# Sliding-window attention on Trainium2: masked-out quarter blocks of the local scores left out of matmul, exp and mask

## The chip, the cores and the metric

One Trainium2 chip, all 8 cores of it. Each core computes two of the sixteen sequences on its own, with the same program; there is no communication. The metric is the device time of one launch in microseconds, that of the slowest core.

## The reference

The input is 16 sequences of 2048 tokens with 1024 features. First comes an attention layer, then a feed-forward part with three pairs of 1024x1024 matrices that are dequantized from 4 bits. The change touches the local attention alone:

```python
def _local_window_attn(Q, K, V):          # 16 heads of 64, window W = 256
    Qb = Q.reshape(Bx, H, nb, W, D)
    ...
    Kw = jnp.concatenate([Kp[:, :, :-1], Kp[:, :, 1:]], axis=3)   # block before, own block
    Vw = jnp.concatenate([Vp[:, :, :-1], Vp[:, :, 1:]], axis=3)
    i = jnp.arange(W)[:, None]
    j = jnp.arange(2 * W)[None, :]
    base = (j > i) & (j <= i + W)
    ...
    sc = jnp.where(mask[None, None], sc, -jnp.inf)
    p = jax.nn.softmax(sc, axis=-1)
    out = jnp.einsum('bhnij,bhnjd->bhnid', p, Vw)
```

Query i of a block of 256 sees keys i+1 to i+256 of the 512 keys of the block before and its own block. A second, pooled ("latent") attention over 64 positions is added with gates, then the output projection and the residual.

## The kernel before

Everything is one program in `build_program`, with one queue per engine and semaphores written out by hand: te counts PE, sc ScalarE (ACT), ve VectorE (DVE). Each engine runs its instructions strictly in the order of the code, so that order is also the order of the work. The first phase (up to about 2014 us) is attention, the second the feed-forward part. The change lies in the first.

The first phase runs over 16 tiles of 256 tokens: `ti` 0 to 15, the first 8 of one sequence, the last 8 of the other. A tile does, in this order: K projection (L461), the latent query projection (L470), gates (L477), pooled keys and values (L557 to L572), the latent attention (scores L622, exp L634, mask L642, product L661, normalized by L678), then the local attention in four groups of four heads, `hf` = 0 to 3, then V and Q projections of the next tile (`emit_vq`, L386 and L415), and the output projection (L893).

Keys lie in chunks of 128: kc = 0, 1 are the block before, kc = 2, 3 the own block. Scores are kept transposed, 128 keys on the partitions and 256 queries along the row. For one `hf`:

- PE, scores (L774): for each kc and each pair of heads two matmuls of 256 query columns into one half (512 columns of f32) of the upper part of psA. Two such halves alternate; the third block waits until the exp of the first has been read out (`t.wait_ge(sc.h, sc0 + nb - 1)`).
- ACT, exp (L796): one 128x512 activation per block, from psA into the buffer expP in SBUF.
- DVE, mask (L808): one 128x512 multiplication per block with the mask `mlocS` of that kc, in place, each followed by a drain (L811) whose end is counted.
- PE, AV (L835, L838): when all masks of the hf are done, for each half of the queries (qc = 0, 1 of 128 each), each of the 4 heads and each kc a matmul of 64 columns with the values and one of 1 column with ones, which sums the row. qc = 0 goes to psB and psC, qc = 1 to psA and psD.

This makes 8 blocks per hf. In tiles 0 and 8, the first of a sequence, there is no block before: kc is only 2 and 3, 4 blocks per hf.

The masks, from the host code, with m1 and m2 triangles of 128x128:

```python
mloc[0] = np.concatenate([m1, zeros_t], axis=1)
mloc[1] = np.concatenate([ones_t, m1], axis=1)
mloc[2] = np.concatenate([m2, ones_t], axis=1)
mloc[3] = np.concatenate([zeros_t, m2], axis=1)
```

What stands between the groups matters too. After the scores, exps and masks of hf = 0 comes `emit_remote_tail`: the latent result is transposed by DMA (SP's queue, L251), projected on PE (L725), copied out by ACT (L736, Copy), and transposed by DMA again. PE's AV of hf = 0 waits for those copies. Then `emit_remgate` on DVE: a wait for the second transposes, and two pairs of gate multiplications (L692, L696); the masks of hf = 1 come behind it in DVE's order. Before hf = 2 stands `emit_ln1_xf` of the next tile: statistics on DVE (L320 to L326), Sqrt on ACT (L337), scaling on DVE (L345, L347), and DMA transposes. ACT loads a table each time that it changes its function (the table load carries the line of the activation behind it). After hf = 3 DVE mixes both attentions, qc = 0 first (L853, L855, L860, L864), then qc = 1; PE goes on with V's projection, 16 matmuls for each half of the tokens (`tc`), where the second half waits for DVE's copies (L397) of the first, and these stand behind the mixing in DVE's order.

Of the kernel before, what the change touches and what calls it, by code (L numbers as in the profile page):

```python
# [11 lines left out]
AF = mybir.ActivationFunctionType  # L12
# [13 lines left out]
TILE = 256  # L26
# [42 lines left out]
def build_program():  # L69
# [30 lines left out]
    with contextlib.ExitStack() as es:  # L100
# [14 lines left out]
        mlocS = sb("mlocS", [128, 4 * 256], BF16)  # L115
# [14 lines left out]
        o_QF = A(H * TILE)  # L130
# [58 lines left out]
        sc = Sem(es, nc, "sc")  # L189
# [51 lines left out]
        def I(sem, inst, k=1):  # L241
            sem.n += k
            inst.then_inc(sem.h, k)
            return sem.n
# [191 lines left out]
        for ti in range(min(B * NT, DBG_A_TILES)):  # L436
# [314 lines left out]
            kc_all = [2, 3] if n == 0 else [0, 1, 2, 3]  # L751
            for hf in range(4):
                if hf == 2 and ti + 1 < B * NT:
                    emit_ln1_xf(ti + 1)
                te_sb = {}
                sc_exp = {}
                sregs = [psA[:, 1024:1536], psA[:, 1536:2048]]

                @block.tensor
                def _(t, hf=hf, slot=slot, pslot=pslot, n=n, kc_all=kc_all):  # L760
                    t.wait_ge(ve.h, kg_evac)
                    sc0 = sc.n
                    nb = 0
                    for kc in kc_all:
                        sl = pslot if kc < 2 else slot
                        koff = (kc % 2) * 128
                        for hg in range(2):
                            reg = sregs[nb % 2]
                            if nb >= 2:
                                t.wait_ge(sc.h, sc0 + nb - 1)  # L770
                            mm = None
                            for hh in range(2):
                                h = hf * 4 + hg * 2 + hh
                                mm = t.matmul(  # L774
                                    reg[:, hh * 256:(hh + 1) * 256],
                                    ar_t.ap()[0:64,
                                              o_KR + h * 2 * W + sl * W + koff:
                                              o_KR + h * 2 * W + sl * W + koff + 128],
                                    ar_t.ap()[0:64,
                                              o_QF + h * TILE:o_QF + (h + 1) * TILE],  # L780
                                    start=True, stop=True)
                            te_sb[nb] = I(te, mm)
                            nb += 1

                nbt = len(kc_all) * 2

                @block.scalar
                def _(s, hf=hf, kc_all=kc_all, nbt=nbt):
                    for nb in range(nbt):
                        s.wait_ge(te.h, te_sb[nb])  # L790
                        reg = sregs[nb % 2]
                        kc = kc_all[nb // 2]
                        hg = nb % 2
                        dst = ar_t.ap()[:, o_expP + kc * 4 * TILE + hg * 2 * TILE:
                                        o_expP + kc * 4 * TILE + (hg + 1) * 2 * TILE]
                        sc_exp[nb] = I(sc, s.activation(dst, reg, AF.Exp))  # L796

                @block.vector
                def _(v, hf=hf, kc_all=kc_all, nbt=nbt):
                    for nb in range(nbt):  # L800
                        v.wait_ge(sc.h, sc_exp[nb])
                        kc = kc_all[nb // 2]
                        hg = nb % 2
                        dst = ar_t.ap()[:, o_expP + kc * 4 * TILE + hg * 2 * TILE:
                                        o_expP + kc * 4 * TILE + (hg + 1) * 2 * TILE]
                        mkv = mlocS.ap()[:, kc * 256:(kc + 1) * 256].unsqueeze(1) \
                            .broadcast_to((128, 2, 256))
                        v.tensor_tensor(dst.rearrange("p (g q) -> p g q", g=2),   # L808
                                        dst.rearrange("p (g q) -> p g q", g=2), mkv,
                                        op=ALU.mult)  # L810
                        I(ve, v.drain())  # L811
                locexp_done = ve.n

                if hf == 0:
                    emit_remote_tail()
                    emit_remgate()

                @block.tensor
                def _(t, hf=hf, slot=slot, pslot=pslot, n=n, kc_all=kc_all):
                    t.wait_ge(ve.h, locexp_done)  # L820
                    if hf == 0:
                        t.wait_ge(ve.h, remnorm_done)
                        t.wait_ge(sc.h, rem_marks['rempf'])
                    for qc in range(QC):
                        avreg = psB[:, 0:1024] if qc == 0 else psA[:, 0:1024]
                        dreg = psC[:, 0:16] if qc == 0 else psD[:, 0:16]
                        for hh in range(4):
                            h = hf * 4 + hh
                            for ki, kc in enumerate(kc_all):
                                st = ar_t.ap()[:, o_expP + kc * 4 * TILE + hh * TILE + qc * 128:  # L830
                                               o_expP + kc * 4 * TILE + hh * TILE + qc * 128 + 128]
                                vsl = (slot * 2 + kc - 2) if kc >= 2 else (pslot * 2 + kc)
                                first = ki == 0
                                last = ki == len(kc_all) - 1
                                mmA = t.matmul(avreg[:, h * 64:(h + 1) * 64], st,  # L835
                                               V(o_VR + vsl * 1024 + h * 64, 64),
                                               start=first, stop=last)
                                mmB = t.matmul(dreg[:, h:h + 1], st,  # L838
                                               onesS[:, 0:1], start=first, stop=last)
                        I(te, mmA)  # L840
                        mix_marks[(hf, qc)] = I(te, mmB)
# [837 lines left out]
```

## Time and profile before

| | us |
|---|---|
| median of the timed runs (2 runs, 4090.43 and 4103.03) | 4096.73 |
| profiled execution, its own time | 4023.44 |
| its span, slowest core (core 3) | 4021.9 |
| spans of the other cores | 4003.5 to 4016.2 |
| PE busy, matmuls | 2496.1 |
| DVE busy | 1923.8 |
| ACT busy | 1168.5 |

The trace is of one execution, on core 3, with times in us from the start of the span. A row of the timeline gives the start, the duration, the engine, the line of the code, output and input by name with their shapes, and in brackets how long the engine stood idle before it and what ended that. xN at the end merges N instructions that follow each other. PEld is the loading of weights, DVEq and ACTq are the drains of those engines. PEclk is the granted clock of TensorE as a share of 2.4 GHz.

### The profile page before, as it was taken

The numbers are of one execution on the slowest core, as the hardware profiler recorded it, in microseconds if no ns is written. First come the engines' busy times: TensorE is split into PE (matmuls) and PEld (weight loads), VectorE is DVE, ScalarE is ACT, GpSimd is POOL, SyncE is SP. The second block draws the span as 40 slices with busy tenths as digits, with TensorE's granted clock in tenths as the row PEclk, the third lists the DMA queues.
The fourth block names the chain that finished last, engine by engine and source line by source line (L and its number), as shares of the span: only waits on it lengthen the run. The fifth ranks groups of instructions, "written<-read, shape, count | busy, mean of one in ns | idle before, by whom it ended". The sixth has DMA issues, their size and how long they took to land.

```text
span 4021.9 us, 57687 instructions; the slowest of 8 cores (4003.5 to 4021.9 us)
## 1 busy us (share of the span) xinstructions
PE 2496.1 (62%) x20176; PEld 1594.7 (40%) x20176; DVE 1923.8 (48%) x3815; ACT 1168.5 (29%) x1873; POOL 88.4 (2%) x142
## 2 busy tenths in 40 slices
PE   0566665666755666665534656758485765848675
PEld 0344433444433444443311434435353443525343
DVE  0455544555544445544423454545444444545454
ACT  0122333222323222233345322313232322323232
POOL 1000000000000000000011000000000000000000
PEclk9767766767665677766656888879787887979788
DMA  9012111112111111111233010010202001020201
GB/s 141 14 30 33 25 30 30 30 30 33 25 35 30 30 30 30 30 27 30 32 86 91 1 35 19 6 48 1 53 1 53 1 17 36 3 51 1 48 1 32
DMA packets 259707, 128.20 MB, mean 32 GB/s; under 512 B 229232, under 2 KB 233504, under 8 KB 259424
## 3 DMA queue, kind: packets, MB, share of 16 engines
q1 hardware_dynamic: 224512, 62.94, 8.8%
q0 software_dynamic: 34912, 61.57, 7.2%
q8 instruction: 167, 2.74, 0.3%
q14 instruction: 116, 0.95, 0.1%
HBM read 61.99 MB, written 25.17 MB: 22 GB/s over the span
## 4 chain that ended last, share of the span: by engine, by line
PE 42%; DVE 26%; ACT 11%; issue 9%; DMA 5%; another core or an unknown queue 2%; DVEq 2%; SPq 1%; ACTq 1%; POOLq 0%; POOL 0%
PE psA L1276 7%; PE psA L1460 5%; PE psB L1460 5%; DMA arena<-arena 3%; ACT arena L796 3%; PE psA L774 3%; DVE arena L1403 3%; DVE arena L1397 3%; DVE arena L1383 2%; PE psA L386 2%; PE psA L461 2%; DVE arena L808 2%; ACT arena L1417 2%; PE psB L893 2%
## 5 line engine op out<-in xcount | busy, mean ns | idle before, releaser
L1276 PE MATMUL psA<-arena,wbig 128*128 128x256 bf16 x3072 | 472.3, 305 | 62.7 <-DVEq L1305 62.6
L1276 PEld LDWEIGHTS psA<-arena,wbig 128*128 128x128 bf16 x3072 | 298.2, 107 | 179.1 <-issue 98.1
L774 PE MATMUL psA<-arena 64*128 64x256 bf16 x960 | 250.7, 392 | 169.9 <-ACT arena L796 169.8
L808 DVE TENSOR_TENSOR arena<-arena,mlocS 128x512 bf16<-128x512 bf16 x480 | 204.1, 425 | 228.2 <-ACT arena L796 204.4
L1302 DVE TENSOR_SCALAR arena<-psA,biasS 128x256 bf16<-128x256 f32 x384 | 185.9, 484 | 246.1 <-PE psA L1282 196.1
L796 ACT ACTIVATE arena<-psA 128x512 bf16<-128x512 f32 x480 | 261.0, 595 | 59.7 <-PE psA L774 58.5
L547 ACT ACT_TABLE_LOAD x16 | 20.5, 1283 | 688.8 <-PE psC L477 688.8
L1460 PE MATMUL psA<-arena,wbig 128*128 128x256 bf16 x1536 | 218.7, 290 | 0.0
L386 PE MATMUL psA<-wbig,arena 128*128 128x512 bf16 x512 | 137.7, 431 | 129.6 <-DMA arena<-arena 120.6
L1460 PE MATMUL psB<-arena,wbig 128*128 128x256 bf16 x1536 | 201.1, 274 | 0.0
L774 PEld LDWEIGHTS psA<-arena 64*128 64x128 bf16 x960 | 73.7, 107 | 319.2 <-issue 309.9
L1417 ACT ACTIVATE arena<-arena,lnbS,lngS 128x256 bf16<-128x256 bf16 x384 | 194.6, 589 | 0.6
L1364 ACT ACT_TABLE_LOAD x48 | 61.6, 1283 | 445.4 <-DVEq L1357 445.3
L1432 PE MATMUL psC<-arena,laS 128*32 128x256 bf16 x384 | 63.4, 320 | 198.8 <-ACT arena L1417 198.8
L835 PE MATMUL psB<-arena 128*128 128x64 bf16 x960 | 80.8, 210 | 146.9 <-DVEq L811 129.7
L1417 ACT ACT_TABLE_LOAD x48 | 61.6, 1283 | 355.9 <-DVEq L1406 355.9
L1460 PEld LDWEIGHTS psA<-arena,wbig 128*128 128x128 bf16 x1536 | 142.3, 103 | 52.4 <-issue 15.3
L1244 PE MATMUL psC<-arena,laS 128*32 128x256 bf16 x384 | 56.5, 296 | 167.8 <-DMA arena<-arena 147.0
L1460 PEld LDWEIGHTS psB<-arena,wbig 128*128 128x128 bf16 x1536 | 134.6, 98 | 36.2
L835 PEld LDWEIGHTS psB<-arena 128*128 128x128 bf16 x960 | 74.3, 122 | 172.7 <-issue 172.7
L1311 ACT ACT_TABLE_LOAD x48 | 61.6, 1283 | 258.6 <-DVEq L1305 258.6
L796 ACT ACT_TABLE_LOAD x64 | 82.1, 1283 | 185.3 <-PE psA L774 184.9
(169 smaller groups left out, 4463.0 us busy)
## 6 DMA issues: line engine op xcount, KB each, us to landing
y<-arena POOLq DMA_DIRECT2D x16, 1024.0 KB, 4.5
arena<-qT POOLq DMA_DIRECT2D x48, 256.0 KB, 2.6
arena<-x_in POOLq DMA_DIRECT2D x16, 512.0 KB, 7.0
x2scr<-arena SPq DMA_DIRECT2D x16, 512.0 KB, 3.0
arena<-x2scr POOLq DMA_DIRECT2D x16, 512.0 KB, 7.7
arena<-arena SPq DMA_TRANSPOSE x224, 3.2
wbig<-wq POOLq DMA_DIRECT2D x1, 2048.0 KB, 18.2
wbig<-wk POOLq DMA_DIRECT2D x1, 2048.0 KB, 29.9
```

The source lines that it names most:

```text
L386: mm = t.matmul(reg, V(o_XF + c * TILE + tc * 128, 128), wv_(o_wv + c * 1024 + og * 512, 512), start=(c == 0), stop=(c == NCH - 1))
L461: mm = t.matmul(reg, wv_(o_wk + c * 1024 + oc * 128, 128), V(o_XF + c * TILE, TILE), start=(c == 0), stop=(c == NCH - 1))
L774: mm = t.matmul(reg[:, hh * 256:(hh + 1) * 256], ar_t.ap()[0:64, o_KR + h * 2 * W + sl * W + koff: o_KR + h * 2 * W + sl * W + koff + 128] ...
L796: sc_exp[nb] = I(sc, s.activation(dst, reg, AF.Exp))
L808: v.tensor_tensor(dst.rearrange("p (g q) -> p g q", g=2), dst.rearrange("p (g q) -> p g q", g=2), mkv, op=ALU.mult)
L835: mmA = t.matmul(avreg[:, h * 64:(h + 1) * 64], st, V(o_VR + vsl * 1024 + h * 64, 64), start=first, stop=last)
L1276: t.matmul(reg, wTv(i0, c, oc * 128, 128), V(hin_o + c * TILE, TILE), start=(c == 0), stop=False)
L1302: v.tensor_scalar(V(y1o + oc * TILE, TILE), Y1REGS[oc % 4], biasS[:, i0 * 8 + oc:i0 * 8 + oc + 1], None, ALU.add)
L1397: v.tensor_tensor(V(y1o, NCH * TILE).rearrange("p (c t) -> p c t", c=NCH), V(y1o, NCH * TILE).rearrange("p (c t) -> p c t", c=NCH), mv, op ...
L1403: v.tensor_tensor(V(go, NCH * TILE).rearrange("p (c t) -> p c t", c=NCH), V(y1o, NCH * TILE).rearrange("p (c t) -> p c t", c=NCH), iv, op= ...
L1417: I(sc, s.activation(V(go + c * TILE, TILE), V(go + c * TILE, TILE), AF.Gelu, bias=lnbS[:, sbk * 8 + c:sbk * 8 + c + 1], scale=lngS[:, sbk ...
L1460: t.matmul(reg, wTv(i1, c, oc * 128, 128), V(go + c * TILE, TILE), start=(c == 0), stop=False)
```

## The change

In chunk 0 the mask is zero for the upper 128 queries, in chunk 3 for the lower 128. The change leaves these parts out everywhere, and multiplies by the mask only where it has a triangle:

- scores: in blocks of kc = 0 and 3 each of the two matmuls has 128 columns instead of 256;
- exp: in those blocks the activation runs over two pieces of 128 (one per head), 128x2x128 instead of 128x512;
- mask: in every block (kc = 0 to 3) only the query half with the triangle is multiplied, 128x2x128 instead of 128x512; the halves of kc = 1 and 2 whose mask is all ones are no longer touched;
- AV: kc = 0 is left out for qc = 1 and kc = 3 for qc = 0, with the `start` and `stop` flags of the sums moved accordingly. Of 64 matmuls per hf 48 stay (in tiles 0 and 8 of 32, 24).

The number of blocks, their order, and all waits and counts stay the same.

```diff
--- before.py
+++ after.py
@@ -764,6 +764,7 @@
                     for kc in kc_all:
                         sl = pslot if kc < 2 else slot
                         koff = (kc % 2) * 128
+                        lq = 0 if kc == 0 else (1 if kc == 3 else None)
                         for hg in range(2):
                             reg = sregs[nb % 2]
                             if nb >= 2:
@@ -771,13 +772,16 @@
                             mm = None
                             for hh in range(2):
                                 h = hf * 4 + hg * 2 + hh
+                                q0c = 0 if lq is None else lq * 128
+                                qn = TILE if lq is None else 128
                                 mm = t.matmul(
-                                    reg[:, hh * 256:(hh + 1) * 256],
+                                    reg[:, hh * 256 + q0c:hh * 256 + q0c + qn],
                                     ar_t.ap()[0:64,
                                               o_KR + h * 2 * W + sl * W + koff:
                                               o_KR + h * 2 * W + sl * W + koff + 128],
                                     ar_t.ap()[0:64,
-                                              o_QF + h * TILE:o_QF + (h + 1) * TILE],
+                                              o_QF + h * TILE + q0c:
+                                              o_QF + h * TILE + q0c + qn],
                                     start=True, stop=True)
                             te_sb[nb] = I(te, mm)
                             nb += 1
@@ -793,7 +797,15 @@
                         hg = nb % 2
                         dst = ar_t.ap()[:, o_expP + kc * 4 * TILE + hg * 2 * TILE:
                                         o_expP + kc * 4 * TILE + (hg + 1) * 2 * TILE]
-                        sc_exp[nb] = I(sc, s.activation(dst, reg, AF.Exp))
+                        if kc in (0, 3):
+                            lq = 0 if kc == 0 else 1
+                            d3 = dst.rearrange("p (g q) -> p g q", g=2)[
+                                :, :, lq * 128:(lq + 1) * 128]
+                            r3 = reg.rearrange("p (g q) -> p g q", g=2)[
+                                :, :, lq * 128:(lq + 1) * 128]
+                            sc_exp[nb] = I(sc, s.activation(d3, r3, AF.Exp))
+                        else:
+                            sc_exp[nb] = I(sc, s.activation(dst, reg, AF.Exp))
 
                 @block.vector
                 def _(v, hf=hf, kc_all=kc_all, nbt=nbt):
@@ -801,13 +813,14 @@
                         v.wait_ge(sc.h, sc_exp[nb])
                         kc = kc_all[nb // 2]
                         hg = nb % 2
+                        mq = 0 if kc in (0, 2) else 1
                         dst = ar_t.ap()[:, o_expP + kc * 4 * TILE + hg * 2 * TILE:
                                         o_expP + kc * 4 * TILE + (hg + 1) * 2 * TILE]
-                        mkv = mlocS.ap()[:, kc * 256:(kc + 1) * 256].unsqueeze(1) \
-                            .broadcast_to((128, 2, 256))
-                        v.tensor_tensor(dst.rearrange("p (g q) -> p g q", g=2), 
-                                        dst.rearrange("p (g q) -> p g q", g=2), mkv,
-                                        op=ALU.mult)
+                        d3 = dst.rearrange("p (g q) -> p g q", g=2)[
+                            :, :, mq * 128:(mq + 1) * 128]
+                        mkv = mlocS.ap()[:, kc * 256 + mq * 128:kc * 256 + mq * 128 + 128] \
+                            .unsqueeze(1).broadcast_to((128, 2, 128))
+                        v.tensor_tensor(d3, d3, mkv, op=ALU.mult)
                         I(ve, v.drain())
                 locexp_done = ve.n
 
@@ -824,14 +837,16 @@
                     for qc in range(QC):
                         avreg = psB[:, 0:1024] if qc == 0 else psA[:, 0:1024]
                         dreg = psC[:, 0:16] if qc == 0 else psD[:, 0:16]
+                        live = [kc for kc in kc_all
+                                if not ((kc == 0 and qc == 1) or (kc == 3 and qc == 0))]
                         for hh in range(4):
                             h = hf * 4 + hh
-                            for ki, kc in enumerate(kc_all):
+                            for ki, kc in enumerate(live):
                                 st = ar_t.ap()[:, o_expP + kc * 4 * TILE + hh * TILE + qc * 128:
                                                o_expP + kc * 4 * TILE + hh * TILE + qc * 128 + 128]
                                 vsl = (slot * 2 + kc - 2) if kc >= 2 else (pslot * 2 + kc)
                                 first = ki == 0
-                                last = ki == len(kc_all) - 1
+                                last = ki == len(live) - 1
                                 mmA = t.matmul(avreg[:, h * 64:(h + 1) * 64], st,
                                                V(o_VR + vsl * 1024 + h * 64, 64),
                                                start=first, stop=last)
```

The sizes on ACT, from the latent exps of tile 1 to the Copy evacuations behind hf = 0 (psA holds the scores, psD the projected latent result), before:

```order
L634 ACTIVATE arena<-psA 64x256 x8
L215 UNCONDITIONAL_BRANCH
L796 ACTIVATE arena<-psA 128x512 x8
L215 UNCONDITIONAL_BRANCH
L736 ACTIVATE arena<-psD 128x128 x2
```

and with the change, the same place:

```order
L634 ACTIVATE arena<-psA 64x256 x8
L215 UNCONDITIONAL_BRANCH
L806 ACTIVATE arena<-psA 128x2x128 x2
L808 ACTIVATE arena<-psA 128x512 x4
L806 ACTIVATE arena<-psA 128x2x128 x2
L215 UNCONDITIONAL_BRANCH
L736 ACTIVATE arena<-psD 128x128 x2
```

The eight exps stay eight, at the same place; the first two and the last two are of the half size. On PE, from the end of AV of hf = 0 to the start of AV of hf = 1 in tile 1, before:

```order
L838 MATMUL psD<-onesS,arena 128x1
L215 UNCONDITIONAL_BRANCH
L774 MATMUL psA<-arena 128x256 x16
L215 UNCONDITIONAL_BRANCH
L835 MATMUL psB<-arena 128x64
```

and with the change:

```order
L853 MATMUL psD<-onesS,arena 128x1
L215 UNCONDITIONAL_BRANCH
L777 MATMUL psA<-arena 128x128 x4
L777 MATMUL psA<-arena 128x256 x8
L777 MATMUL psA<-arena 128x128 x4
L215 UNCONDITIONAL_BRANCH
L850 MATMUL psB<-arena 128x64
```

Nothing changes its place here either; the outer blocks have narrower matmuls. The lines of the changed kernel behind the scores are shifted: L774 is L777, L796 is L806 and L808, L808 is L823, L835 is L850, L838 is L853.

## Rows read from the trace of the kernel before

**Rows 1.** The page of the kernel before: its span and the engines' busy time.

```profile
span 4021.9 us, 57687 instructions; the slowest of 8 cores (4003.5 to 4021.9 us)
...
PE 2496.1 (62%) x20176; PEld 1594.7 (40%) x20176; DVE 1923.8 (48%) x3815; ACT 1168.5 (29%) x1873; POOL 88.4 (2%) x142
```

**Rows 2.** Groups by line: shape, count | busy us, mean ns | idle before, releaser.

```profile
L796 ACT ACTIVATE arena<-psA 128x512 bf16<-128x512 f32 x480 | 261.0, 595 | 59.7 <-PE psA L774 58.5 <-issue 0.3
...
L774 PE MATMUL psA<-arena 64*128 64x256 bf16 x960 | 250.7, 392 | 169.9 <-ACT arena L796 169.8
...
L808 DVE TENSOR_TENSOR arena<-arena,mlocS 128x512 bf16<-128x512 bf16 x480 | 204.1, 425 | 228.2 <-ACT arena L796 204.4 <-issue 23.9
...
L634 ACT ACTIVATE arena<-psA 64x256 bf16<-64x256 f32 x128 | 41.3, 372 | 18.1 <-PE psA L622 17.9
...
L642 DVE TENSOR_TENSOR arena<-arena,mlatS 64x256 bf16<-64x256 bf16 x128 | 36.2, 283 | 121.9 <-ACT arena L634 108.8 <-issue 13.1
...
L563 PE MATMUL psD<-wbig,arena 128*8 128x128 bf16 x256 | 29.9, 311 | 0.0
```

**Rows 3.** Timeline, tile 5, hf = 2 and 3: start us, us, engine line.

```profile
805.55 1.09 ACT L796 ACTIVATE arena<-psA 128x512 bf16<-128x512 f32 x2
...
806.29 1.07 PE L774 MATMUL psA<-arena 64*128 64x256 bf16 x4 [2.91 <-ACT arena L796]
...
806.97 1.09 ACT L796 ACTIVATE arena<-psA 128x512 bf16<-128x512 f32 x2 [0.33 <-PE psA L774]
...
811.12 0.42 DVE L808 TENSOR_TENSOR arena<-arena,mlocS 128x512 bf16<-128x512 bf16 x1 [0.19 <-ACT arena L796]
...
811.72 0.21 PE L835 MATMUL psB<-arena 128*128 128x64 bf16 x1 [1.52 <-DVEq L811]
...
814.35 1.03 PE L774 MATMUL psA<-arena 64*128 64x256 bf16 x4
...
816.33 1.09 ACT L796 ACTIVATE arena<-psA 128x512 bf16<-128x512 f32 x2
```

**Rows 4.** Timeline, hf = 0 of tile 0, then hf = 0 to 2 of tile 5.

```profile
182.00 1.09 ACT L796 ACTIVATE arena<-psA 128x512 bf16<-128x512 f32 x2
...
185.43 1.01 PE L725 MATMUL psD<-arena,wbig 128*128 128x256 bf16 x4 [1.62 <-DMA arena<-arena]
...
771.51 1.09 ACT L796 ACTIVATE arena<-psA 128x512 bf16<-128x512 f32 x2
...
776.16 1.01 PE L725 MATMUL psD<-arena,wbig 128*128 128x256 bf16 x4
...
777.25 1.28 ACT L736 ACT_TABLE_LOAD   x1 [0.39 <-PE psD L725]
...
791.42 0.17 DVE L692 TENSOR_TENSOR rr<-glgrT,rden 128x16 f32<-128x16 f32 x1 [13.90 <-DMA arena<-arena]
...
794.83 0.43 DVE L808 TENSOR_TENSOR arena<-arena,mlocS 128x512 bf16<-128x512 bf16 x1 [0.19 <-issue]
...
799.12 0.42 DVE L808 TENSOR_TENSOR arena<-arena,mlocS 128x512 bf16<-128x512 bf16 x1 [0.19 <-issue]
...
804.04 0.20 ACT L337 ACTIVATE sigv<-stat 128x1 f32<-128x1 f32 x1 [0.66 <-DVEq L329]
```

**Rows 5.** Timeline, end of tile 4: mixing (DVE) and V projection (PE).

```profile
702.90 0.26 DVE L853 RECIPROCAL rl<-psC 128x16 f32<-128x16 f32 x1 [1.79 <-PE psC L838]
...
703.84 4.77 PE L386 MATMUL psA<-wbig,arena 128*128 128x512 bf16 x16
...
709.27 3.40 PE L386 MATMUL psA<-wbig,arena 128*128 128x512 bf16 x15 [0.66 <-DVE arena L397]
```

**Rows 6.** Windows, core 3: length, busy of PE, PEld, DVE, ACT, POOL, clock, DMA share, GB/s.

```profile
825.00:829.00 4.00, 4.00 (x16) 1.52 (x14) 3.52 (x6) 0.00 (x0) 0.00 (x0) 0.50 0.00 0
...
829.00:861.00 32.00, 28.14 (x232) 22.21 (x230) 20.78 (x47) 0.00 (x0) 0.00 (x0) 1.00 0.18 34
...
889.00:946.00 57.00, 33.69 (x369) 18.59 (x370) 23.88 (x54) 29.93 (x56) 0.00 (x0) 0.56 0.20 24
```

## The prediction

> **What bounds the kernel now.** I read the page's totals first, then the groups by line, then the timeline of tile 5 in order of time, then the windows for the granted clock. No engine is busy for more than 62% of the 4021.9 us span (PE) or 48% (DVE) [rows 1]. So a removed instruction is worth something only where its engine is the one that the next stage waits for, and the timeline has to say where that is. All that the change touches lies in the 64 head groups of the attention part (16 tiles, 4 groups hf = 0 to 3 each). 14 tiles have all four key chunks (I call them full), tiles 0 and 8 only chunks 2 and 3. Each group is a string of scores, exp, mask and AV, but which link of it the next stage waits for differs from group to group.
>
> The string in hf = 2 and 3 of tile 5 [rows 3]. Exps come in pairs; a pair takes 1.09 us and the next starts 1.42 us after it (805.55 to 806.97). The reader is to see why: PE may refill a PSUM half only when its exp has ended, so a period is one exp (0.60), 0.14 to PE's start at 806.29, and 0.68 for two matmuls until the next exp at 806.97. Four pairs make this 5.35 us. The last mask starts at 811.12, 5.57 us after the first exp, and ends 6.00 after it; AV starts 0.17 us later (released by DVE's drain), its 64 matmuls take until 814.35, 40 ns each, and the next group's scores and table load follow until the exp at 816.33.
>
> hf = 0 and 1 are tied otherwise [rows 4]. In hf = 0 the path leaves the exps early: L725 follows the last scores in PE's own order (776.16), and ScalarE's Copy evacuations wait for it (0.39 us at 777.25); masks and AV of hf = 0 are covered. Then DVE waits 13.90 us for the transposes (791.42), does four gate operations and only then the 8 masks of hf = 1, 0.613 us apart (794.83 to 799.12, 7 steps), while their exps are long done: DVE is the path. AV of hf = 1 is covered, since the LN statistics follow on DVE and the exps of hf = 2 wait for Sqrt, which waits for DVE (804.04).
>
> Behind hf = 3 the path is DVE again, not PE [rows 5]: the mixing starts at 702.90 when the first half of AV (qc = 0) is done, and V's second half (709.27) waits 0.66 us for DVE's copy. That is 6.4 us from the start of the mixing, the pattern repeats at each of the 15 changes of tile, and the second half of AV is covered by it.
>
> **The change part by part.** The new sizes do not stand in the trace, so each is bounded. *Exp, 2x128 instead of 512 elements:* 595 ns for 512, 372 ns for 256 at L634, on 64 partitions [rows 2]. Ends: 298 (half) and 595 (the two pieces cost as before). I take 372, the nearest row: same function, same PSUM source. *Mask, 2x128:* 425 ns for 512, 283 for 256 at L642 [rows 2]. Ends: 212 and 425. From the two durations of that kind I take 0.29, so 0.48 with the 0.19 between masks instead of 0.613: 0.13 less. *Scores, two matmuls of 128 columns:* L563 has 311 ns for 128 columns, L774 392 for 256 [rows 2]. At the 0.50 clock of this stage [rows 6] 128 columns are 107 ns, so two matmuls give 0.21 at most, 0 at least; I take 0.20. *AV:* of 64 matmuls 16 go, at 40 ns 0.64 us, 0.32 of it in the qc = 0 half; in tiles 0 and 8 half of that. No DMA and no wait is added, and each semaphore count stays.
>
> The string with these numbers, from the first exp on, for hf = 2 or 3 of a full tile: exp 2 at 0.37+0.14+0.68 = 1.20; exp 4 at 1.20+1.42 = 2.62; exp 6 (half scores) at 2.62+0.60+0.14+0.48 = 3.84; its mask at 3.84+0.37+0.10 = 4.31, the last mask at 4.80, its end 5.09. Before 6.00: **0.91 less**. The sum per full tile:
> hf = 0: first scores 0.20, then the last score block may start when exp 5 has ended, 0.22 earlier, and is itself 0.20 shorter: 0.62. This stays on the path only if the transposes that L725 needs have landed. In tile 0, with its short hf = 0, they are late: L725 waits 1.62 us for them [rows 4] and starts 3.4 us after the first exp (185.43 - 182.00); in tile 5 it starts 4.65 us after (776.16 - 771.51). 0.62 fits into the 1.2 us between.
> hf = 1: 8 masks x 0.133 = 1.07.
> hf = 2: 0.91, and AV 0.64: 1.55. Its first scores are covered by the LN statistics.
> hf = 3: first scores 0.20, 0.91, AV's qc = 0 half 0.32: 1.43.
> Together 4.67 us, x 14 = 65.4. Tiles 0 and 8: hf = 0 nothing (transposes), hf = 1 4 x 0.133 = 0.53, hf = 2 0.68+0.32, hf = 3 0.68+0.16, together 2.37, x 2 = 4.7 (0.68 is the same string with two pairs). The last tile has no LN of a next tile between, so AV of hf = 1 and the first scores count there: 0.64+0.20 = 0.8. **Sum 70.9, say 71 us.** The projections and the whole second phase are untouched.
>
> What is costed at nothing: AV of hf = 0 and 1 (14 x about 1.2 us) is hidden by DVE's wait for the transposes and by the masks and LN statistics; the second AV half of hf = 3 by DVE's mixing; the masks of hf = 0 by the Copy evacuations. Were those covers gone, some 21 us more would come (rival 3).
>
> The profiled execution took 4023.4 us, and its span is the base of this sum; the median of the timed runs is 4096.7, 1.8% more. 71 us of the former is 1.76%. I take the same 71 us off the median: **4026 us**.
>
> A rule on ScalarE's price. By the Trainium skill (ScalarE: Activation LUTs, What ACT_TABLE_LOAD costs) an ACTIVATE with immediate operands takes 186 ns and 0.833 ns per element, so 399 ns for 256 and 613 for 512. The row for 512 says 595, so the rule is a little high here. By it the exps would give some 2 us less in all.
>
> **The rivals.**
> 1. Masks cost as before (425 ns): the fixed part or the two pieces eat the half. Against it: 283 ns at L642. Then hf = 1 loses 1.07 and hf = 2 and 3 0.27 each: 3.06 per full tile, in all 46 us: 4050.
> 2. Exps cost 595 ns in two pieces. For it: no strided activation that reads PSUM stands in my rows. The last exp then comes at 4.55, the last mask ends at 5.54 (0.46 less), hf = 0 gives 0.40: 3.55 per full tile, in all 54 us: 4042.
> 3. The covered parts count too: 0.6 (AV of hf = 0), 0.64 and 0.32 more per full tile, 21 us: 92 us, 4005. Against it stand DVE's 13.90 us wait and V's 0.66 us wait for DVE [rows 4, 5].
> 4. Slower: the clock. In attention PE is granted 0.56 of full speed (889 to 946), at the head of the V projection still 0.50 (825 to 829), and 1.00 from there (829 to 861) [rows 6]; PE was busy without a gap for 4.00 us before it rose, and AV ran directly ahead of that. With a quarter of AV gone and shorter scores the rise could come later in each tile. K and output projections (64 matmuls of 256 columns) would need 107 ns a matmul at 2.4 GHz (1.00) and 213 at 1.2 GHz (0.50), so each would take 6.8 us more, Q and V by my estimate some 8 together: 21 us per tile if the clock never rose, 315 us in all, 4341. Break-even with my 4.67 us is a rise about 9 us later in each tile. Against it: V's 32 dense matmuls follow without a gap in any case, and the first half of V has spare time behind DVE's mixing.
> That half speed is the default and sustained activity releases it is also what the Trainium skill says (TensorE: Matmul & The Clock Gate, Part 1, the HAM clock gate). The trace agrees, 0.50 then 1.00; the rule speaks for rival 4 as a direction, not as a size.
>
> **How the numbers follow.** Forecast 0.65, rival 1 0.07, rival 2 0.10, rival 3 0.14, rival 4 0.04. A measurement here tells about 2% from no change, 82 us. Of the forecast's own spread (scores' 0.20 and the spread of the medians, 4090 to 4103) some 0.08 lies beyond 82 us, with rival 3 that is 0.22 faster; 0.04 slower; 0.74 within 2%. The forecast's own range is 4010 to 4045; the range given holds rivals 1 to 3 and the scatter of a median: 3998 to 4068. All upper prices at once would leave only AV's share, some 14 us (4083), which I leave out.
>
> **What would show it.** The group of half exps at about 372 ns, masks at 0.29 us with starts 0.48 apart in hf = 1 (3.85 us for eight, now 4.72), last mask 5.1 us after the first exp in hf = 2 and 3, AV in 48 matmuls and 2.0 us; V's second half still 6.4 us behind the mixing's start; L725 in full tiles released by PE's order and not by a DMA; tile period shorter by 4.7 us; second phase unchanged. I am wrong if the half operations cost over 0.45 us, if L725 turns to waiting for the transposes, or if the window behind V's start shows 0.50 for longer than now.

## The result and the profile after

The changed kernel took **3991.76 us** in the median of 18 runs, against 4025.28 us for the kernel before in 17 runs of the same rounds: ratio 0.987, 95% interval 0.9835 to 0.9904. That is faster, by less than 2%. Some executions of either kernel run with one die or both at a lower granted clock (about 0.70 to 0.745 in place of 0.75) and take up to 2.7% longer: 12 of the 18 of the changed kernel here against, by their times, 5 of the 17 of the kernel before, and 2 of 6 against 5 of 16 in the second timing, so the medians include them, the ratios leave out the clearest, and where a profile has one only the other die is compared. The six shortest times of the changed kernel (3948 to 3959 us) and the twelve shortest of the kernel before (4020 to 4030) are 68 us apart by their medians; why the first timing of the changed kernel has so many longer ones stays open. In a second timing (below) it was 3956.2 against 4022.3 us, ratio 0.9818, 0.9761 to 0.9876; the intervals overlap.

4026 us had been predicted, with a range from 3998 to 4068. The measured time lies 6 us below the range. The gain itself had been put at 71 us; the medians differ by 33.5 and 66 us, the spans of the profiles by 65 and 71 us.

The page of the changed kernel, the totals:

```profile
span 3954.3 us, 55767 instructions; the slowest of 8 cores (3942.1 to 3954.3 us)
...
PE 2424.0 (61%) x19216; PEld 1563.6 (40%) x19216; DVE 1859.8 (47%) x3815; ACT 1124.1 (28%) x1873; POOL 88.5 (2%) x142
```

The spans by core (core 0 is the shortest, core 3 the longest):

```profile
core 0: 3942.1 us, clock 0.757
...
core 3: 3954.3 us, clock 0.751
...
die 0 (median of its cores): 3947.5 us, clock 0.754
...
die 1 (median of its cores): 3946.0 us, clock 0.754
```

The mean of the eight spans is 3947.0 us; before it was 4011.9 us: 64.9 us less. PE lost 72 us of busy time, DVE 64 and ACT 44 [rows 1], 180 us in all, for 65 us of time.

The groups by line with the shapes kept apart (line, engine, operation, shapes, count | busy us, mean ns | idle before); they answer to [rows 2]:

```profile
L808 ACT ACTIVATE arena<-psA 128x512 bf16<-128x512 f32 x240 | 130.4, 595 | 49.1 <-PE psA L777 49.0
...
L806 ACT ACTIVATE arena<-psA 128x256 bf16<-128x256 f32 x240 | 86.2, 384 | 15.5 <-PE psA L777 0.8
...
L823 DVE TENSOR_TENSOR arena<-arena,mlocS 128x256 bf16<-128x256 bf16 x480 | 140.4, 292 | 218.8 <-ACT arena L806 105.2 <-ACT arena L808 82.4 <-issue 31.2
...
L777 PE MATMUL psA<-arena 64*128 64x256 bf16 x480 | 123.3, 395 | 145.8 <-ACT arena L806 122.4 <-ACT arena L808 23.4
...
L777 PE MATMUL psA<-arena 64*128 64x128 bf16 x480 | 79.2, 288 | 46.8 <-ACT arena L808 39.1
```

The exp in two pieces takes 384 ns (taken: 372), the mask 292 (taken: 290), a matmul of 128 columns is 107 ns shorter than one of 256. The profile shows the two pieces merged as 128x256.

The timeline of tile 5, hf = 2 and the start of hf = 3, answering to [rows 3]:

```profile
789.88 0.66 ACT L806 ACTIVATE arena<-psA 128x256 bf16<-128x256 f32 x2
...
791.08 1.09 ACT L808 ACTIVATE arena<-psA 128x512 bf16<-128x512 f32 x2 [0.55 <-PE psA L777]
...
794.68 0.29 DVE L823 TENSOR_TENSOR arena<-arena,mlocS 128x256 bf16<-128x256 bf16 x1 [0.20 <-ACT arena L806]
...
795.15 0.21 PE L850 MATMUL psB<-arena 128*128 128x64 bf16 x1 [1.05 <-DVEq L824]
...
797.14 0.61 PE L777 MATMUL psA<-arena 64*128 64x128 bf16 x4
797.61 1.28 ACT L806 ACT_TABLE_LOAD   x1 [3.03 <-PE psA L777]
798.90 0.66 ACT L806 ACTIVATE arena<-psA 128x256 bf16<-128x256 f32 x2
```

From the first exp (789.88) to the end of the last mask (794.97) it is 5.09 us, as forecast; before it was 6.00. AV with its 48 matmuls lasts from 795.15 to 797.14, 2.0 us instead of 2.6, and the next first exp follows the scores after 1.76 us instead of 1.98.

hf = 0 and 1 of tile 5, answering to [rows 4]:

```profile
763.78 1.28 ACT L736 ACT_TABLE_LOAD   x1 [0.57 <-PE psD L725]
...
776.81 0.18 DVE L692 TENSOR_TENSOR rr<-glgrT,rden 128x16 f32<-128x16 f32 x1 [13.20 <-DMA arena<-arena]
...
780.22 0.29 DVE L823 TENSOR_TENSOR arena<-arena,mlocS 128x256 bf16<-128x256 bf16 x1 [0.19 <-ACT arena L806]
...
783.58 0.29 DVE L823 TENSOR_TENSOR arena<-arena,mlocS 128x256 bf16<-128x256 bf16 x1 [0.19 <-issue]
```

ACT still waits for L725 behind hf = 0 (0.57 us). DVE still waits 13.20 us for the transposes, and the masks of hf = 1 still stand in a row behind the gates, now 0.48 us apart: 780.22 to 783.87 is 3.65 us, before 4.72.

From tile 5 to tile 6, answering to [rows 5]:

```profile
805.48 0.26 DVE L868 RECIPROCAL rl<-psC 128x16 f32<-128x16 f32 x1 [1.48 <-PE psC L853]
...
806.10 5.38 PE L386 MATMUL psA<-wbig,arena 128*128 128x512 bf16 x16
...
811.86 3.61 PE L386 MATMUL psA<-wbig,arena 128*128 128x512 bf16 x16 [0.38 <-DVE arena L397]
```

V's second half starts 6.38 us after the mixing, as before (6.37), and still waits for DVE (0.38 us). From the mixing of the last tile to the end of the program it is 2003.2 us in the mean of the cores in both kernels: the second phase did not change.

### The profile page after: what moved, and what is told of

It is laid out like the page before. It is cut to its first block, busy times and chain, and to the rows that moved or that the text cites. A ratio compares the mean times of both kernels' runs of the same rounds, so it can differ in the third digit from the quotient of the medians.

```text
span 3954.3 us, 55767 instructions; the slowest of 8 cores (3942.1 to 3954.3 us)
## 1 busy us (share of the span) xinstructions
PE 2424.0 (61%) x19216; PEld 1563.6 (40%) x19216; DVE 1859.8 (47%) x3815; ACT 1124.1 (28%) x1873; POOL 88.5 (2%) x142
## 4 chain that ended last, share of the span: by engine, by line
PE 42%; DVE 26%; ACT 10%; issue 10%; DMA 6%; another core or an unknown queue 2%; DVEq 2%; SPq 1%; ACTq 1%; POOLq 0%; POOL 0%
PE psA L1291 8%; PE psA L1475 5%; PE psB L1475 5%; DMA arena<-arena 4%; DVE arena L1418 3%; DVE arena L1412 3%; PE psA L777 2%; PE psA L461 2%; DVE arena L1398 2%; PE psA L386 2%; ACT arena L1432 2%; PE psB L908 2%; ACT L1379 2%; PE psA L1297 2%
## 5 line engine op out<-in xcount | busy, mean ns | idle before, releaser
L1291 PE MATMUL psA<-arena,wbig 128*128 128x256 bf16 x3072 | 477.2, 307 | 53.6 <-DVEq L1320 53.6
L777 PE MATMUL psA<-arena 64*128 64x128 bf16 (+1 forms) x960 | 202.5, 342 | 192.6 <-ACT arena L806 122.4
L823 DVE TENSOR_TENSOR arena<-arena,mlocS 128x256 bf16<-128x256 bf16 x480 | 140.4, 292 | 218.8 <-ACT arena L806 105.2
L1475 PE MATMUL psA<-arena,wbig 128*128 128x256 bf16 x1536 | 219.6, 291 | 0.0
L777 PEld LDWEIGHTS psA<-arena 64*128 64x128 bf16 x960 | 75.0, 110 | 306.1 <-issue 293.5
L808 ACT ACTIVATE arena<-psA 128x512 bf16<-128x512 f32 x240 | 130.4, 595 | 49.1 <-PE psA L777 49.0
L850 PE MATMUL psB<-arena 128*128 128x64 bf16 x704 | 61.4, 210 | 132.5 <-DVEq L824 115.4
L386 PEld LDWEIGHTS psA<-wbig,arena 128*128 128x128 bf16 x512 | 54.5, 111 | 211.0 <-issue 172.8
L461 PE MATMUL psA<-arena,wbig 128*128 128x256 bf16 x1024 | 115.6, 274 | 24.7 <-DVEq L923 21.8
```

What stands on the lines that cost most here:

```text
L386: mm = t.matmul(reg, V(o_XF + c * TILE + tc * 128, 128), wv_(o_wv + c * 1024 + og * 512, 512), start=(c == 0), stop=(c == NCH - 1))
L461: mm = t.matmul(reg, wv_(o_wk + c * 1024 + oc * 128, 128), V(o_XF + c * TILE, TILE), start=(c == 0), stop=(c == NCH - 1))
L777: mm = t.matmul(reg[:, hh * 256 + q0c:hh * 256 + q0c + qn], ar_t.ap()[0:64, o_KR + h * 2 * W + sl * W + koff: o_KR + h * 2 * W + sl * W + ...
L823: v.tensor_tensor(d3, d3, mkv, op=ALU.mult)
L1291: t.matmul(reg, wTv(i0, c, oc * 128, 128), V(hin_o + c * TILE, TILE), start=(c == 0), stop=False)
L1475: t.matmul(reg, wTv(i1, c, oc * 128, 128), V(go + c * TILE, TILE), start=(c == 0), stop=False)
```

## The experiments

Each run but the last has a profile and rounds of timing beside the kernel before on the same chip; the last is a profile only. In most full tiles the stretches between the marks (first exp, last mask, AV) repeat within hundredths of a microsecond (in a few tiles the strings of hf = 2 and 3 are up to 0.4 us longer, in every run), so the trace tells small terms far better than the timed runs. "Mean span" is the mean over eight cores of that run's profile. Means over the full tiles are worked out from the traces of all eight cores, too (of die 1 alone where the table says so).

| run | mean span, us | to 4011.9 | ratio of times, 95% interval |
|---|---|---|---|
| the change, first profile | 3947.0 | -64.9 | 0.987, 0.9835 to 0.9904 |
| the change again | 3940.9 | -71.0 | 0.9818, 0.9761 to 0.9876 |
| inner masks alone | 3999.9 (die 1) | -10.8 (die 1; before 4010.7) | 0.9966, 0.9933 to 1.0 |
| AV alone | 3991.8 | -20.1 | 0.9949, 0.9923 to 0.9976 |
| scores and exps | 3991.0 | -20.9 | 0.9954, 0.9925 to 0.9983 |
| exps alone | 3997.2 | -14.7 | 0.9962, 0.9934 to 0.999 |
| the change, full masks | 3972.6 | -39.3 | 0.9911, 0.988 to 0.9943 |
| kernel before, gates late | 3956.8 | -55.2 | 0.9833, 0.9744 to 0.9922 |
| the change, gates late | 3878.9 | -133.0 | 0.9657, 0.9569 to 0.9744 |
| kernel before, again | 4014.4 (die 1) | +3.7 (die 1) | profile only |

### Masks of the inner chunks alone

```diff
+                        if kc in (1, 2):
+                            mq = 0 if kc == 2 else 1
+                            d3 = dst.rearrange("p (g q) -> p g q", g=2)[
+                                :, :, mq * 128:(mq + 1) * 128]
...
+                            v.tensor_tensor(d3, d3, mkv, op=ALU.mult)
+                        else:
...
```

Expected: 

> The kernel before, with only the masks of key chunks 1 and 2 halved (240 of the 480, 4 of 8 per group). My theory (masks are on the path in hf = 1 alone, where eight stand in a row behind the gates): 4 x 0.132 = 0.53 us per full tile and 0.26 in tiles 0 and 8, 8 us in all; hf = 1's mask string of 4.72 us becomes 4.19, the string from first exp to last mask in hf = 2 and 3 stays 6.0 us. Rival (masks count in every group): three or four times as much, 22 to 30 us.

The timeline of core 3, tile 5: masks of hf = 1, then first exp and last mask of hf = 2:

```profile
795.48 0.42 DVE L816 TENSOR_TENSOR arena<-arena,mlocS 128x512 bf16<-128x512 bf16 x1 [0.19 <-issue]
...
796.71 0.29 DVE L812 TENSOR_TENSOR arena<-arena,mlocS 128x256 bf16<-128x256 bf16 x1 [0.19 <-ACT arena L796]
...
799.24 0.43 DVE L816 TENSOR_TENSOR arena<-arena,mlocS 128x512 bf16<-128x512 bf16 x1 [0.19 <-issue]
...
805.66 0.60 ACT L796 ACTIVATE arena<-psA 128x512 bf16<-128x512 f32 x1
...
811.23 0.43 DVE L816 TENSOR_TENSOR arena<-arena,mlocS 128x512 bf16<-128x512 bf16 x1 [0.19 <-ACT arena L796]
```

Of the eight masks in a row, those of kc = 1 and 2 (four) are short, and the row lasts from 795.48 to 799.67, 4.19 us, as expected. In hf = 2 the distance from first exp to the end of the last mask is 6.00 us, unchanged: there short inner masks gain nothing, since the next exps come later anyway. Per full tile only hf = 1 moved, by 0.54 us. The spans are compared on die 1; their 10.8 us agrees with 8 us, within the scatter of a profile (last experiment), and not with the rival's 22. The timed 0.3% cannot decide, since its interval reaches 1.0.

### AV alone

```diff
+                        live = [kc for kc in kc_all
+                                if not ((kc == 0 and qc == 1) or (kc == 3 and qc == 0))]
...
-                            for ki, kc in enumerate(kc_all):
+                            for ki, kc in enumerate(live):
```

Expected: 

> The kernel before, with only the zero blocks left out of AV (64 matmuls per group become 48). My theory (AV counts whole in hf = 2, half in hf = 3, not at all in hf = 0 and 1): 0.64 + 0.32 = 0.96 us per full tile, half of it in tiles 0 and 8, 0.64 more in the last tile: 15 us in all. Rival (the covered AV parts count too): 2.2 us per full tile, 33 us in all.

AV of hf = 2 in tile 5, core 3, first matmul of AV and first matmul of the next scores:

```profile
808.43 0.21 PE L837 MATMUL psB<-arena 128*128 128x64 bf16 x1 [1.52 <-DVEq L811]
...
810.42 0.82 PE L774 MATMUL psA<-arena 64*128 64x256 bf16 x3
```

1.99 us, before 2.63. Per full tile the step from last mask to next first exp lost 0.64 us in hf = 2 and the step to the mixing 0.32 us in hf = 3; the strings, masks and V's second half stayed. In hf = 1 of the last tile, which has no LN statistics behind it, AV gave another 0.64 us, as forecast. The sum of such steps is the forecast 15 us; the spans differ by 20 us, so most of the other 5 are scatter between profiles. The rival's 33 us is excluded. One covered part counted a little all the same: from the last Copy evacuation to the first gate, a wait for the second transposes, it was 5.22 us in the mean of the full tiles in place of 5.32. The other runs without these AV matmuls (5.21 to 5.23, where the gates stand in their old place) and those with them (5.31 to 5.33) show the same difference; 0.10 us a tile is 1.4 us in all, and why was not tried.

### Scores and exps, and exps alone

```diff
+                        lq = 0 if kc == 0 else (1 if kc == 3 else None)
...
-                        sc_exp[nb] = I(sc, s.activation(dst, reg, AF.Exp))
+                        if kc in (0, 3):
...
+                            sc_exp[nb] = I(sc, s.activation(d3, r3, AF.Exp))
```

The second kernel has `lq = None` in the scores, so that all score matmuls keep 256 columns.

Expected with both: 

> The kernel before, with only scores and exps of chunks 0 and 3 narrowed; masks at 128x512 and AV with 64 matmuls. My theory: hf = 0 gives 0.48 us, hf = 1 nothing, hf = 2 and 3 give 0.63 each from first exp to last mask (6.0 to 5.4 us) and hf = 3 another 0.21 ahead of its first exp: 1.95 us per full tile, 28 us in all. Rival (the string is paced by the masks once exps are short): 0.3 or less from first exp to last mask, 15 us in all.

Expected with exps alone: 

> The kernel before, with only the exps of chunks 0 and 3 narrowed to 128x2x128; scores, masks and AV as before. Theory: 0.22 us in hf = 0 and 0.42 each in hf = 2 and 3 from first exp to last mask (6.0 to 5.6 us): 1.06 us per full tile, 16 us in all, so that the narrower scores are worth the other 12 us of the run with both. Rival (two pieces cost as much as 512 elements): no gain, exps at 595 ns.

The timeline of the run with both, hf = 2 of tile 5, on its slowest core (core 2):

```profile
806.63 0.66 ACT L806 ACTIVATE arena<-psA 128x256 bf16<-128x256 f32 x2
...
809.96 0.43 DVE L820 TENSOR_TENSOR arena<-arena,mlocS 128x512 bf16<-128x512 bf16 x1 [0.38 <-ACT arena L808]
...
810.47 0.87 ACT L806 ACTIVATE arena<-psA 128x256 bf16<-128x256 f32 x2
...
810.58 0.42 DVE L820 TENSOR_TENSOR arena<-arena,mlocS 128x512 bf16<-128x512 bf16 x1 [0.19 <-ACT arena L808]
...
811.19 0.42 DVE L820 TENSOR_TENSOR arena<-arena,mlocS 128x512 bf16<-128x512 bf16 x1 [0.19 <-issue]
...
811.80 0.42 DVE L820 TENSOR_TENSOR arena<-arena,mlocS 128x512 bf16<-128x512 bf16 x1 [0.19 <-issue]
```

**Here my expectation failed.** From the first exp (806.63) to the end of the last mask (812.22) it is 5.59 us: 0.4 gained, not 0.63. The last exps are ready (both run from 810.47 to 811.34), but the masks at 810.58, 811.19 and 811.80 follow each other at their own pace of 0.613 us, the last two with the drain alone between (issue). I had let the mask of exp 6 start when that exp had ended, and forgotten that the mask of exp 5 still holds DVE. This is what the rival says, the masks pace the string once the exps are short; its size, 0.3 us or less, was too small. With exps alone the same distance is 5.59 us too: narrower scores give nothing inside the string as long as the masks are long. They give 0.21 us ahead of the first exp of hf = 0 and of hf = 3 and some hundredths in hf = 0. Both runs lie where this puts them, 21 and 15 us below in mean span.

### The change with full masks

```diff
-                        d3 = dst.rearrange("p (g q) -> p g q", g=2)[
-                            :, :, mq * 128:(mq + 1) * 128]
...
+                        mkv = mlocS.ap()[:, kc * 256:(kc + 1) * 256].unsqueeze(1) \
+                            .broadcast_to((128, 2, 256))
```

Expected: 

> The changed kernel, with its masks put back to 128x512 (as in the kernel before). My theory: scores, exp and AV give 1.95 + 0.96 us per full tile, 43 us in all against the kernel before, so that the masks' share of the change is some 23 us: 1.07 in hf = 1 and 0.27 each in hf = 2 and 3. If the parts add up, this run is e2 and e3 together. Rival (the masks are hidden but for hf = 1): the run lies 15 us above the changed kernel, not 23.

39.3 us below the kernel before, 25.6 and 31.7 above the two profiles of the change, where 23 had been expected. The parts add up: AV alone 20.1 and scores with exps 20.9 make 41.0. The masks' share per full tile is 1.07 us in hf = 1 and 0.49 in each of hf = 2 and 3 (first exp to last mask 5.6 against 5.1 us), not 0.27: short exps and short masks need each other there. The rival (masks count in hf = 1 alone, 15 us) is excluded by these strings.

### The gates behind hf = 2

```diff
                 if hf == 2 and ti + 1 < B * NT:
                     emit_ln1_xf(ti + 1)
+                if hf == 3:
+                    emit_remgate()
...
                 if hf == 0:
                     emit_remote_tail()
-                    emit_remgate()
```

Expected, on the changed kernel: 

> The changed kernel, with the four gate operations (emit_remgate) issued on DVE behind the masks of hf = 2 instead of ahead of those of hf = 1. Theory (in hf = 1 DVE waits for the transposes and the gates while the exps are done, and behind hf = 2 it has over 4 us to spare): the stretch from the last Copy evacuation to the last mask of hf = 1 falls from 12.3 to about 8.8 us, 3.5 us per full tile, 4.8 in tiles 0 and 8, 58 us in all below the changed kernel: some 3890 us against 4015 for the kernel before. hf = 3's first mask stays 0.5 us behind its first exp. Rival (the transposes are what is waited for and the wait moves along): gain under 10 us.

Expected, on the kernel before: 

> The kernel before, with emit_remgate moved in the same way. Theory: the same stretch falls from 13.4 to about 10.2 us, 3.1 us per full tile, 4.5 in tiles 0 and 8, 52 us in all below the kernel before. The change on top of it (e5 against e6) is then worth 75 us instead of 67, since in hf = 1 AV of hf = 0, first scores and the exp string come onto the path in place of the eight masks in a row. Rival: the gates were not what held hf = 1, and the time stays within 10 us.

The changed kernel with late gates, tile 5 of core 3 (its masks are L825, its exps L808 and L810):

```profile
745.53 0.62 ACT L736 ACTIVATE arena<-psC 128x128 bf16<-128x128 f32 x2 [0.23 <-PE psC L725]
...
748.10 1.28 ACT L808 ACT_TABLE_LOAD   x1 [1.95 <-PE psA L779]
...
749.88 0.29 DVE L825 TENSOR_TENSOR arena<-arena,mlocS 128x256 bf16<-128x256 bf16 x1 [12.49 <-ACT arena L808]
...
754.20 0.29 DVE L825 TENSOR_TENSOR arena<-arena,mlocS 128x256 bf16<-128x256 bf16 x1 [0.20 <-ACT arena L808]
...
765.45 0.29 DVE L825 TENSOR_TENSOR arena<-arena,mlocS 128x256 bf16<-128x256 bf16 x1 [0.19 <-ACT arena L808]
...
765.99 0.18 DVE L692 TENSOR_TENSOR rr<-glgrT,rden 128x16 f32<-128x16 f32 x1 [0.26 <-issue]
...
767.99 1.22 DVE L696 TENSOR_TENSOR arena<-arena,rr 128x1024 bf16<-128x1024 bf16 x1
...
770.15 0.29 DVE L825 TENSOR_TENSOR arena<-arena,mlocS 128x256 bf16<-128x256 bf16 x1 [0.94 <-ACT arena L808]
```

The last Copy evacuation ends at 746.15, the masks of hf = 1 now run beside their exps (749.88 to 754.49): from that evacuation to the last mask 8.3 us, in tile 5 of the changed kernel 11.8; in the mean of the full tiles 8.5 in place of 12.3, 3.8 us less (3.5 expected). The gates stand at 765.99 to 769.21, begun 0.26 us after the last mask of hf = 2 with no wait for the transposes, and the first mask of hf = 3 comes at 770.15, 0.49 us behind its exp: they are hidden whole. On the changed kernel this gives 68 us in mean span (62 to 68, by which profile of the change is taken), on the kernel before 55 us (the stretch is 3.4 us shorter there, 13.4 to 10.0). The version with both beats both kernels: 3936.61 us in the median and 3887.33 at best, ratio 0.9657, 0.9569 to 0.9744. By the spans the change is worth 78 us on top of late gates (3956.8 to 3878.9), 75 had been expected.

### The change again, and the kernel before again

Both are unchanged kernels, so there is no edit. Expected of the changed kernel: 

> The changed kernel once more, in the same rounds as the others. The profile's spans gave 65 us less (mean of eight cores), 1.6%; the first timing gave a ratio of 0.987. If the trace tells the gain rightly, undisturbed executions lie 60 to 70 us below those of the kernel before. If narrower matmuls cost something that the trace does not show, the difference stays at 50 us or less here too.

66 us by the medians, 71 by the spans. The interval of the ratio is 50 to 96 us, so a gain of 50 us stands just at its edge; the spans of both profiles (65 and 71 us) speak against a price that the stretches do not show.

Expected of the kernel before: 

> The kernel before, profiled a second time, to see how far one profile of the same program differs from another. In every run so far the stretch between K's projection and the latent result is 0.15 to 0.3 us per full tile longer than in the one profile of the kernel before, and V's fast clock starts 0.4 us later. If that is scatter of one profile, this one shows it too and its eight spans lie up to 5 us above 4012 in the mean. If it is a price of the change (rival 4 in small), this profile repeats the first within 0.1 us per tile.

The spans of die 1 in that profile:

```profile
core 4: 4020.7 us, clock 0.751
...
core 5: 4013.8 us, clock 0.753
...
core 6: 4013.7 us, clock 0.750
...
core 7: 4009.2 us, clock 0.752
```

Their mean is 4014.4 us, against 4010.7 in the first profile. Measured tile by tile on this die, the stretch from the start of K's projection to the latent result is 41.00 us in the mean of the full tiles, 0.45 more than in the first profile, though nothing was changed. The changed kernel's two profiles have 41.00 and 40.83 on all cores against 40.67, so what seemed to be given back there is scatter of single profiles, and not a price of the change. (The expectation says that every run so far showed it; the runs with the inner masks alone and AV alone did not, 40.61 and 40.56.) V's fast clock is another matter. It starts 2.4 us after V in the mean of the full tiles of the first profile, 2.5 in this one and 3.0 in both profiles of the changed kernel: this part repeats, and belongs to the change. What it costs stands below, at rival 4.

## Why the prediction was wrong, and where it was right

**The step that failed is the base.** "I take the same 71 us off the median" took it off 4096.7 us, the median of two runs. Fifteen more runs put the median of the same kernel at 4025.28 us, and 12 of the 17 lie between 4020 and 4031; the two I had, 4090 and 4103 us, are among the five above 4070. Why those five ran longer the trace of the profiled execution could not show. The profiled execution, 4023.4 us, was the better base, and the text named the 1.8% between them without asking why. 4023.4 - 70.9 = 3952.5 us; the changed kernel's profiled execution took 3955.8 and its second median was 3956.2. The range was drawn round the same wrong base, and its lower end gave way by 6 us. That the miss is only 34 us is luck: the base was 71 us too high, and the median of the 18 runs, 3991.76, lies 37 us above 4025.3 - 70.9 = 3954.4, since it includes 12 longer executions.

**The sum** was 70.9 us; the profiles show 64.9 and 71.0. By its terms, per full tile (mean over the cores, first profile of the change against the first of the kernel before):

| term | predicted | measured |
|---|---|---|
| hf = 0, up to L725 | 0.62 | 0.52 |
| hf = 1, masks in a row | 1.07 | 1.07 |
| hf = 2, string | 0.91 | 0.87 |
| hf = 2, AV | 0.64 | 0.64 |
| hf = 3, first scores | 0.20 | 0.21 |
| hf = 3, string | 0.91 | 0.87 |
| hf = 3, half of AV | 0.32 | 0.32 |
| sum | 4.67 | 4.50 |

With tiles 0 and 8 and the last tile these terms make some 69 us, between the two profiles. The period of a full tile became 4.2 and 4.4 us shorter where 4.7 had been forecast; most of the rest is the scatter ahead of the latent result.

Hf = 0 is short by 0.10 us. The spare time before the transposes was thinner than I put it; the line L725 shows what it waited for, in us and times:

```profile
  DMA arena<-arena: 6.0, 5
```

before 3.2 us in 2 tiles, the first of each sequence; now three full tiles have it too. In the mean of all full tiles and cores the wait is 0.11 us, before 0.01. Tile 13 waits on all eight cores in every run with narrowed scores (0.25 to 0.54 us) and on none in the other runs, so it is not chance; why the transposes land later in some tiles was not tried. "L725 turns to waiting for the transposes" was a sign of being wrong in the prediction, and it came true in this small measure.

Two smaller slips of the working: in tiles 0 and 8 the whole saving of AV, 8 matmuls, lies in the qc = 0 half, so hf = 3 gives 0.32 us there and not 0.16; and the row of masks forecast at 3.85 us counts eight periods, while the 4.72 it stands beside runs from the first start to the last end (3.65 after the change, 1.07 less, as the sum had it).

**Rival 1 and 2** (masks or exps as dear as before) are excluded by 292 and 384 ns. Rival 1's price was wrong as well: with full masks the strings lose 0.49 us each, not 0.27. **Rival 3** (the covered parts count) is excluded by the run with AV alone: in hf = 0 and 1, ahead of the last tile, only the wait for the second transposes moved, by 0.10 us. **Rival 4**, the clock. The windows of the changed kernel for the same places as [rows 6], from V's start on:

```profile
806.90:810.50 3.60, 3.60 (x12) 1.39 (x11) 3.12 (x6) 0.00 (x0) 0.00 (x0) 0.61 0.00 0
...
810.50:842.00 31.50, 27.62 (x229) 21.95 (x227) 20.26 (x46) 0.00 (x0) 0.00 (x0) 1.00 0.18 35
...
870.00:925.00 55.00, 31.23 (x325) 18.15 (x325) 21.22 (x56) 26.96 (x56) 0.00 (x0) 0.53 0.17 25
```

PE is granted 0.61 in the 3.6 us from 806.9 to 810.5, 1.00 for the projections, 0.53 in attention. One tile does not show the rise well, as it comes 0.5 to 4.7 us after V's start, from tile to tile. In the mean of the full tiles and cores it comes 2.4 us after V's start before the change and 3.0 after it, and the kernel before, profiled again, has 2.5. AV alone gives 2.8, scores with exps 2.7, exps alone 2.4, and with late gates it is 2.2 without the change and 2.9 with it. So the second sign of being wrong, 0.50 for longer behind V's start, came true too, in small: V's first half takes 5.05 us in place of 4.75. It cost nothing, because V now starts 0.32 us sooner after the mixing (0.71 in place of 1.03 us) and its second half waits for DVE in any case: it starts 6.4 us after the mixing in every run. The Trainium skill's rule (TensorE: Matmul & The Clock Gate, Part 1) that activity releases the slow clock agrees in direction, with less work on PE ahead of V and a later rise; rival 4 failed by its price.

The price of an exp from the Trainium skill (ScalarE: Activation LUTs, What ACT_TABLE_LOAD costs), 399 ns for 256 elements, stands against 384 measured: 15 ns too high, where the 372 that I took from the row on 64 partitions was 12 too low. For 512 elements it stays above too (613 against 595).

## What to carry to other kernels

Read the gain on the path and not from the busy time: 180 us of work left three engines and 65 us of time went, and the places that paid could be named beforehand, stretch by stretch. Where two engines pace a string in turn (exps and masks here), shorten both, or the second takes over at once; and when a row of cheap instructions stands behind a wait on an in-order queue, look at moving the wait: here it gave 55 to 68 us, nearly as much as all the trimming. Take the base of a forecast from the execution whose trace you read, and ask why timed runs differ from it before you trust a median of two.

## What was not expected of the hardware

An activation over two pieces of 128 elements took 384 ns where one piece of 256 on 64 partitions took 372, so a split access costs little. In a row of masks, and at the end of a string once the exps are short, the masks' pace of 0.613 us decides and not their duration of 0.425: between two masks 0.19 us pass with nothing to wait for (issue), and these gaps are a third of a row of masks.

A table load of 1.28 us stands ahead of the first exp of every head group, 64 of them in each kernel. The section on the kernel tells of loads where ACT changes its function; they also stand where it does not, as between the exps of hf = 2 and those of hf = 3. Before the change, in tile 5:

```profile
815.04 1.28 ACT L796 ACT_TABLE_LOAD   x1 [4.14 <-PE psA L774]
```

It starts when the first scores are ready (815.04), and the exp follows it at 816.33; in the changed kernel it is 797.61 and 798.90. In hf = 3 it is thus on the path. Without it 16 x 1.28, some 20 us, would be gained there, by an estimate from these rows; no run tried it, nor what puts the load there.
